# Four products straight into TensorE's accumulator in every second group of states, in place of GpSimd's pair sums

## The reference

```python
def step(h, inputs):
    dt_t, B_t, C_t, x_t = inputs
    dA = jnp.exp(dt_t[..., None] * A)
    h = h * dA + (dt_t * x_t)[..., None] * B_t[:, None, :]
    y = jnp.einsum('bds,bs->bd', h, C_t)
    return (h, y)
```

## Time and profile before

| what | value |
|---|---|
| median of 3 runs | 2714.99 us (2712.98 to 2716.85) |
| profiled execution, its own time | 2713.94 us |
| its span in the trace | 2712.1 us |
| first scan starts, last scan starts | 39.67 us, 336.91 us |
| last `ysum` starts | 342.11 us |
| chunks by their first scan | 39.67, 105.63, 179.19, 259.56 us |
| busy over the whole span | PE 87%, DVE 90%, ACT 85%, POOL 57% |
| granted TensorE clock, mean over the span | 0.952 of full |

### The profile page before, as it was taken

The page is one execution under the profiler, slowest core; times in us unless marked ns, Lnnn a source line. Parts: engine busy times, 40 slices in busy tenths (PEclk is TensorE's granted clock), DMA queues, the critical chain, the costliest instruction groups (busy, mean ns, idle before and its releaser), DMA issues.

```text
span 2712.1 us, 93622 instructions
## 1 busy us (share of the span) xinstructions
PE 2355.8 (87%) x38225; PEld 1247.0 (46%) x38225; DVE 2436.3 (90%) x3370; ACT 2299.3 (85%) x4209; POOL 1535.4 (57%) x2901
## 2 busy tenths in 40 slices
PE   7777587799989998999999999999999999999866
PEld 3444376244444444444444444444444444444345
DVE  5888745799999999999999999999999999999988
ACT  6888544699999999999999999999999999998853
POOL 5878765444664456644664456545664466544544
PEclk8888788699999999999999999999999999999988
DMA  3222233112110111011110101011111101010000
GB/s 111 76 82 74 70 98 108 50 49 64 33 38 31 49 50 47 24 45 44 53 35 34 49 32 55 30 49 41 40 35 50 49 32 41 28 49 11 2 2 16
DMA packets 52141, 127.23 MB, mean 47 GB/s; under 512 B 6017, under 2 KB 40705, under 8 KB 47233
## 3 DMA queue, kind: packets, MB, share of 16 engines
q1 hardware_dynamic: 43329, 113.12, 12.4%
q0 software_dynamic: 2432, 5.08, 0.6%
q10 hardware_dynamic: 5952, 3.04, 0.4%
HBM read 96.09 MB, written 29.18 MB: 46 GB/s over the span
## 4 chain that ended last, share of the span: by engine, by line
PE 39%; issue 18%; ACT 12%; DVE 12%; POOL 11%; DMA 1%; ACTq 0%; SPq 0%; POOLq 0%; DVEq 0%
PE bank L780 12%; PE bank L707 12%; PE bank L791 10%; ACT E L1073 9%; DVE NM L1507 7%; ACT acc L1024 1%; POOL hC L1652 1%; POOL acc L1769 1%; POOL H L1779 1%; PE bank L688 1%; POOL H L1782 1%; POOL smp L1762 1%; ACT UB L1035 1%; PE bank L701 1%; POOL hC L1655 1%
## 5 line engine op out<-in xcount | busy, mean ns | idle before, releaser
L1507 DVE TENSOR_REDUCE NM<-bank 128x1 f32<-128x1024 f32 x1536 | 1798.4, 1206 | 80.1 <-PE bank L780 59.4
L1073 ACT ACTIVATE E<-bank,NM 128x1024 f32<-128x1024 f32 x1536 | 1707.5, 1118 | 165.7 <-DVE NM L1507 139.2
L780 PE MATMUL bank<-KS,QS 72*32 72x512 bf16 x12288 | 960.0, 388 | 163.9 <-ACT E L1073 110.5
L791 PE MATMUL bank<-E,dg 128*32 128x256 f32 x12288 | 926.2, 385 | 1.7 <-ACT acc L1024 1.7
L1831 POOL TENSOR_TENSOR dg<-mask,RZ 128x128 f32<-128x128 f32 x384 | 153.0, 398 | 827.0 <-DVE RZ L1517 726.8
L780 PEld LDWEIGHTS bank<-KS,QS 72*32 72x32 bf16 x12288 | 252.0, 96 | 707.7 <-ACT E L1073 586.1
L791 PEld LDWEIGHTS bank<-E,dg 128*32 128x32 f32 x12288 | 385.1, 111 | 292.9 <-issue 63.0
L1073 ACT ACTIVATION_READ_ACCUMULATOR E<-bank,NM 128x1 f32 x1536 | 310.5, 202 | 0.0
L1769 POOL TENSOR_TENSOR acc<-acc,rel 128x256 f32<-128x256 f32 x384 | 272.4, 730 | 7.8 <-ACT acc L1024 7.8
L707 PE MATMUL bank<-H,ET 128*32 128x129 f32 x6144 | 187.9, 273 | 2.5 <-DVE ET L1448 2.5
L707 PE MATMUL bank<-hT,WL 128*32 128x256 f32 x2304 | 163.3, 387 | 23.0 <-ACT UB L1035 19.4
(11 more groups left out here) (292 smaller groups left out, 2669.3 us busy)
## 6 DMA issues: line engine op xcount, KB each, us to landing
QS<-scratch SPq DMA_DIRECT2D x69, 384.0 KB
KS<-scratch SPq DMA_DIRECT2D x22, 1152.0 KB
scratch<-UB SPq DMA_DIRECT2D x144, 128.0 KB
CB<-crows SPq DMA_DIRECT2D x32, 512.0 KB, 3.7
WL<-in_wl SPq DMA_DIRECT2D x6, 1091.0 KB, 21.3
KS<-scratch SPq DMA_DIRECT2D x6, 384.0 KB
first<-in_fill SPq DMA_DIRECT2D x8, 247.5 KB, 4.0
second<-in_fill SPq DMA_DIRECT2D x8, 247.5 KB, 4.2
```

Source lines behind the costliest of these rows:

```text
L780: inst = PE_.matmul(bank[x % 3][32 * i:32 * i + 32, k * 512:k * 512 + 512], QS[0:72, half % 2, 4 * hq + i, r0:r0 + 32], KS[0:72, b, k, 4 * ...
L791: inst = PE_.matmul(pb(6)[32 * k:32 * k + 32, 256 * grp:256 * grp + 256], dg[:, x // 4 % 3, x % 4, :], E[:, x % NE, :].rearrange("p (i k c ...
L1073: A_.activation(E[:, x % NE, :], bank[x % 3][:, :], ACT.Exp, bias=NM[:, x % 4:x % 4 + 1], accum_out=ZS[:, quad % 3, j:j + 1]).then_inc(s[" ...
L1507: V.tensor_reduce(NM[:, x % 4:x % 4 + 1], bank[x % 3][:, :], AX.X, ALU.max, negate=True).then_inc(s["rowmax"], 1)
```

## The change

The 128 steps are 32 groups of four. In the even groups nothing changes. In the odd ones (`whole`) GpSimd makes no pair sum, and TensorE adds each of the four products itself, five steps after the product's own. Who makes which product stays as it was. There are 32 pair sums fewer, and 32 more identity matmuls (96 in place of 64).

```diff
+def whole(q):
+    return q % 2 == 1
...
+def paired(n):
+
+    return n // 8 * 2 + n % 2 + 1
...
 def summed(n):
-    return n // 4 * 2 + n % 2 + 1
+    return sum(4 if whole(q) else 2 for q in range(n // 4)) + (n % 4 if whole(n // 4) else n % 2) + 1
+
+def sums_at(p):
+    out = []
+    for n in range(max(p - 7, 0), min(p - 2, CSTEPS)):
+        late = 5 if whole(n // 4) else {0: 6, 1: 7}.get(n % 4)
+        if late == p - n:
+            out.append(n)
+    return out
...
-                e.wait_ge(s["two"], summed(n))
+                if whole(n // 4):
+                    name, count = product_of(n)
+                    e.wait_ge(s[name], count)
+                else:
+                    e.wait_ge(s["two"], paired(n))
...
-                for late, at in ((6, 0), (7, 1)):
-                    if 0 <= p - late < CSTEPS and (p - late) % 4 == at:
-                        ysum(p - late)
+                for n in sums_at(p):
+                    ysum(n)
...
-                    e.wait_ge(s["y"], summed(32 * k + 28 + c))
+                    e.wait_ge(s["y"], summed(32 * k + 30 + c))
...
-                    e.wait_ge(s["mulP"], made("POOL", n))
-                    e.wait_ge(s["mulC"], made("DVE", n - 2))
-                    G.tensor_tensor(hC[:, (n - 2) % 8, :], hC[:, (n - 2) % 8, :], hC[:, n % 8, :], ALU.add).then_inc(s["two"], 1)
+                    if not whole(n // 4):
+                        e.wait_ge(s["mulP"], made("POOL", n))
+                        e.wait_ge(s["mulC"], made("DVE", n - 2))
+                        G.tensor_tensor(hC[:, (n - 2) % 8, :], hC[:, (n - 2) % 8, :], hC[:, n % 8, :], ALU.add).then_inc(s["two"], 1)
```

More of the change, by code:

```diff
@@ L101, in carried, with ours @@
     return p // 64 * 32 + p % 32 + 1
+def whole(q):
+    return q % 2 == 1
+def ours(engine, q):
+    if engine == "DVE":
+        return (0, 1)
+    return (2, 3)
 def made(engine, n):
-    ours = (0, 1) if engine == "DVE" else (2, 3)
-    return n // 4 * 2 + sum(i <= n % 4 for i in ours)
+    return sum(len(ours(engine, q)) for q in range(n // 4)) + sum(i <= n % 4 for i in ours(engine, n // 4))
 def product_of(n):
-    engine = "DVE" if n % 4 < 2 else "POOL"
+    engine = "DVE" if n % 4 in ours("DVE", n // 4) else "POOL"
     return ("mulC" if engine == "DVE" else "mulP"), made(engine, n)
+def paired(n):
+    return n // 8 * 2 + n % 2 + 1
 def summed(n):
-    return n // 4 * 2 + n % 2 + 1
+    return sum(4 if whole(q) else 2 for q in range(n // 4)) + (n % 4 if whole(n // 4) else n % 2) + 1
[6 more added lines that the diff above has]
+    return out
 def in_order(engine, k):
@@ L608, in ysum @@
                 k, c = n // 32, n % 2
-                e.wait_ge(s["two"], summed(n))
+                if whole(n // 4):
[3 more added lines that the diff above has]
+                    e.wait_ge(s["two"], paired(n))
                 if n % 32 < 2 and k:
                     e.wait_ge(s["y2"], 2 * (k - 1) + c + 1)
-                PE_.matmul(pb(c), ident[:, :], hC[:, n % 8, :], start=(n % 32 < 2), stop=(n % 32 >= 28)).then_inc(s["y"], 1)
+                PE_.matmul(pb(c), ident[:, :], hC[:, n % 8, :], start=(n % 32 < 2), stop=(n % 32 >= 30)).then_inc(s["y"], 1)
             chosen = {}
@@ L1224, in scan_dve @@
                     expert_dve(e, own, j, x)
-                if 0 <= p - 1 < CSTEPS and (p - 1) % 4 < 2:
+                if 0 <= p - 1 < CSTEPS and product_of(p - 1)[0] == "mulC":
                     mul_c(p - 1)
@@ L1645, in scan_pool @@
                 n = p
-                if 0 <= n < CSTEPS and n % 4 >= 2:
+                if 0 <= n < CSTEPS and product_of(n)[0] == "mulP":
                     g = n // 2
```

## The result

| comparison, on its chip | before, median us | change, median us (lowest to highest) | ratio, 95% interval |
|---|---|---|---|
| first | 2714.36 | 2700.75 (2690.43 to 2702.48) | 0.9944 [0.9929, 0.9959] |
| second (e4_change_again) | 2716.29 | 2696.98 (2695.47 to 2707.57) | 0.9940 [0.9921, 0.9958] |
| third (e14_change_fourth) | 2733.93 | 2720.84 (2717.19 to 2727.56) | 0.9952 [0.9938, 0.9967] |

The first row's median of before is over six runs, the three of the table ahead among them. The change is faster by about 0.55%, 13 to 16 us. The forecast was 7.3 us, half of that. The direction was right.

A forecast was written before the change was run, and what follows sets the result against it. No engine was taken to bound the whole recurrence; a removed pair sum counts only where GpSimd ends a wait. Terms -5.6 - 2.7 + 4.0 - 2.0 - 1.0 + 0 = -7.3 us gave 2707 us; own range 2704 to 2711, wider 2700 to 2714.5.

The forecast's parts named there:

- (a): Starts of chunks 1 and 2: no pair sums ahead of `xa`, 2.8 us won each time, 5.6 us gain.
- (b): Behind those waits at chunks 1 and 2: TensorE's clock stays higher, 0.8 and 1.9 us won, 2.7 us gain.
- (c): Convolution steps: two added `ysum`s a chunk at 0.86 us cost 5.2, less one 1.20 us wait: +4.0 us.
- (d): Gating in chunk 3: VectorE's small operations no longer held up behind GpSimd's pair sums, -2.0 us.
- (e): Transposes of `U`, steps 28 and 29: TensorE less idle ahead, so less `ysum` time at the lower clock, -1.0 us.
- (f): End of the recurrence: four pair sums go, but TensorE does more `ysum`s behind step 121; 0 us.
- (g): Elsewhere: added `ysum`s lie in TensorE's gaps and removed sums in GpSimd's slack; counted as nothing.
- clock rival: Chunk 2, B projection: added `ysum`s keep TensorE's clock up, a 5.27 us wait goes; -12.6 us, 2702; chance 0.17.
- slower rival: TensorE becomes the bound: added `ysum`s on the path, also at steps 17 to 20; +8.9 us, 2723; chance 0.10.

The follow-up runs named there:

- e4_change_again: The change itself, unaltered, run again on the same chip as three other kernels, against the kernel before: ratio 0.9940, 2696.98 us.
- e14_change_fourth: The change itself, unaltered, in a third comparison with the kernel before and a fourth trace: ratio 0.9952, 2720.84 us.
- e2: The change in groups 7 and 15 alone, the other odd groups keeping their pair sums as in the kernel before: ratio 0.9967, 9 us.
- e7: Kernel before without the odd groups' pair sums and with no matmul added, so 32 of 128 products are missing from y: ratio 0.9933, 18 us.
- e6: Kernel before with all its pair sums, plus the 32 matmuls the change adds, fed with zeros: ratio 1.0009, 2.4 us slower, not clear of no change.
- e12: The change in groups 1, 3, 9, 11 and 17 alone, in and just behind the convolution steps, otherwise the kernel before: ratio 0.9993.
- e9: Kernel before with the pair sums of group 19 alone (steps 76 to 79) left out, two of 128 products missing: ratio 0.9979, 5.7 us.
- e10: The change in groups 13, 19 and 21 alone, otherwise the kernel before: ratio 0.9981.
- e1: The change in 11 of its 16 groups; groups 1, 3, 9, 11 and 17 keep their pair sums as in the kernel before: ratio 0.9949.
- e3: The change in groups 25, 27, 29 and 31 alone (last chunk), otherwise the kernel before: ratio 0.9983, 4.6 us.

## Why the prediction was half right

**(a) and (b), the chunk starts: right.** 8.3 us forecast, 8.9 measured, in all four traces to 0.1 us, and e2 gives them alone. The split was less good: 3.6 and 4.7 were forecast for the two chunks and both gave 4.45. The relief is enough for it: e7 adds no matmul and wins the same, with 1.39 us of wait left at `trx` and its transposes there in 0.63 us where they took 0.94. So the clock comes with the shorter wait.

The added matmuls by themselves win 1.3 us in chunk 1 (e6) and nothing in chunk 2, and the most of the 1.3 is not the clock. Scan 36 comes only 0.45 us sooner after scan 35. The other 0.9 us lie between scans 36 and 38, where VectorE's product comes to stand just ahead of a GpSimd sum and no longer just behind one. Before, then e6:

```profile
120.20 1.73 DVE L1203 TENSOR_TENSOR hC<-CB,hs 128x512 f32<-128x512 f32 x1
```

```profile
123.19 0.67 DVE L1205 TENSOR_TENSOR hC<-CB,hs 128x512 f32<-128x512 f32 x1
```

In the change too 0.4 of chunk 1's 4.45 us lie between scans 36 and 38, where this product takes 1.22 us. Step (b) had put all but the sums' 2.8 us down to the clock.

**(c), the convolution steps: the failed step.** Two things were wrong in it, with opposite signs. "GpSimd's relief is worth nothing there but for the 1.20 us wait" was false. It was argued from the earlier trace rows, where TensorE has no gap, but those rows show TensorE as it ran with late chunk starts. +3.9 was forecast in three stages, +2.4 measured (+1.4, +2.15, -1.2), and the groups alone (e12) cost nothing that the time shows. The price of 0.86 us for an added matmul held where it could be read alone (scans 48 to 50); what the relief saves was missing. The other thing is the matmul of step 17, "covered" in the prediction: it cost 0.96 us in chunk 0 and 0.86 in chunk 1, a term of 1.8 us that was put at nothing. The relief's worth in these stages is therefore larger than the 1.5 us by which the sum of (c) is off.

**(d), VectorE behind GpSimd: failed in the gating, true elsewhere.** Scans 100 to 120 take 54.66 us before and 54.77 in the change, so -2.0 was 0: the waits moved. (Over four traces each the means are 54.9 and 54.5, by one trace of before at 55.7 and one of the change at 53.7.) In the change, GpSimd and then VectorE:

```profile
265.96 1.27 POOL L1681 TENSOR_TENSOR hC<-CB,hs 128x512 f32<-128x512 f32 x1 [0.27 <-DVE hs L1247]
```

```profile
255.84 1.18 DVE L1360 TENSOR_TENSOR GM<-GM,cst 128x64 f32<-128x64 f32 x1
...
266.03 1.27 DVE L1360 TENSOR_TENSOR GM<-GM,cst 128x64 f32<-128x64 f32 x1
```

The operation of the earlier trace rows again takes 1.27 us, now beside a product that began 0.07 us ahead of it and ended 0.07 us ahead of its end. The Trainium skill, SBUF — State Buffer, Who interferes with whom, has the second to come blocked for the whole of the first one's instruction; these rows agree, and they show what the prediction's reading of the rule left out, that a product of GpSimd takes the sum's place. In chunk 2 the same relief did win: from scan 78 to 80 e9 is 1.7 to 2.0 us shorter than the traces of before.

**(e), the transposes of U: the number came by luck.** Scans 90 to 100 take 21.2 us before and 20.0 in the change, -1.1 where -1.0 was forecast. But the transposes of `U` (steps 28 and 29) belong to scans 92 to 95, which take 7.65 to 7.82 us before and 7.55 to 7.81 in the change, and e10, which has the group that is summed just ahead of them, takes 21.1 us for scans 90 to 100, as before. All of the 1.1 us is between scans 99 and 100, 3.65 us before and 2.52 in the change. There VectorE has two operations of 128x64; before, both stand behind a GpSimd instruction:

```profile
266.29 1.20 DVE L1329 TENSOR_TENSOR GM<-GL,VT 128x64 f32<-128x64 f32 x1
267.52 1.31 DVE L1331 TENSOR_TENSOR GM<-GM,cst 128x64 f32<-128x64 f32 x1
```

and in the change only the second (1.18 us at 255.84, above):

```profile
255.62 0.20 DVE L1358 TENSOR_TENSOR GM<-GL,VT 128x64 f32<-128x64 f32 x1
```

That is (d)'s mechanism at a place where (d) had counted nothing. e1 and e7 have this gain, e2, e3 and e10 have not, so it goes with the pair sums of group 23 (or of group 5, the only other one that they add).

**(f), the end: mis-sized.** 0 forecast, -1.5 measured (-2.6 in e3). The five `ysum`s come as one block behind the wait, to be read against the earlier trace rows:

```profile
326.14 5.97 PE L642 MATMUL bank<-hC,ident 128*128 128x512 f32 x10 [2.68 <-POOL hC L1685]
331.95 0.38 PE L709 MATMUL bank<-ident,WAX 128*128 128x128 f32 x2
```

and in e3, with a granted clock of 1.00 from 334 to 340 us (in the change it was 0.50 from 326 to 328):

```profile
335.81 4.56 PE L642 MATMUL bank<-hC,ident 128*128 128x512 f32 x10 [2.68 <-POOL hC L1685]
340.21 0.38 PE L709 MATMUL bank<-ident,WAX 128*128 128x128 f32 x2
```

The prediction compared 7.1 us before with 6.8 to 8.5 after, at 1.7 us for each of the first three. They took 4.6 to 6.3 us in all, and the waits of 0.65 and 0.49 us that before had between its last three, for pair sums, are gone. Before's own four traces lie between 6.66 and 7.28 us here.

**(g), the rest: open.** "The removed sums [lie] in GpSimd's slack" was taken as 0; the stages 50 to 66 and 84 to 90 show -1.45 and -1.1. Both lie within the scatter of before's own traces (2.3 and 4.3 us), so what part is real stays open; e10 and e12 put 50 to 66 at -0.3 and -0.7 alone. At one place the words are shown false: scans 78 to 80 are 1.4 to 1.7 us shorter in the change, as the sum of step 78 had been in VectorE's way (e9); scans 80 to 82 give 0.86 of that back.

**The rivals.** The clock rival was nearest in size (-12.6 us), but for a wrong reason, and so by luck: its 5.3 us were a wait that is 2.1 us long in the second trace of before, and the scan behind it came 2.0 to 3.6 us sooner in the three repeats. In its place stand the small gains above: against the terms, (a) and (b) give 0.6 more, (c) 1.5, (f) 1.5, and the stages counted as nothing 2.5, with 1.4 less from (d) and (e) together. Of the slower rival's sum two things held: the price of the matmul, and that the one of step 17 is on the path in chunks 0 and 1.

What stays open: the traces account for 12.1 of the 13 to 16 us. These 12.1 us are a ratio of 0.9955, which lies inside all three intervals of the result, so that a further gain behind the scan is not shown. The time from the last `ysum` on varies from 2367.9 to 2373.1 us in before's own traces. Which of the gains of (c) belong to which pair sum was not tested either, as e12 took five groups at once.

## What to carry to other kernels

Relief of an engine must be priced for the state after the edit: when an earlier wait goes, the next stage meets its partners less ready, and relief that the old trace shows as worthless (no gap) then saves the give-back. Removing one instruction of a pair that blocks another engine gains only if nothing takes its place; half of it mostly moved the collisions (1.6 us won from scan 90 to 120), all of it won 7.8 us there. And profile the same kernel several times before a term rests on one wait: a stage of identical code differed here by up to 4.3 us from trace to trace.

## What was not expected of the hardware

- TensorE's granted clock fell at different instructions in executions of the same program. In chunk 2 it was at 0.51 from 224 us on in one trace and still 1.00 until 228 in another; ahead of the fall TensorE had waited 2.45 and 1.58 us. The trace with a wait of 2.21 us kept the upper level through the projection as well. The stage in which it falls (scans 84 to 90) was 18.74 to 23.03 us long in four traces of the kernel before.
- 32 added matmuls of 128x512, 27.5 us at 0.86 each, cost 2.9 us of the scan against the mean of before's traces and 0.09% [-0.01, 0.19] of the time (e6). The start of chunk 1 was even 1.3 us shorter with them, mostly as a VectorE product no longer met a GpSimd sum.
- A cast of 128x128 by VectorE takes 0.20 us alone (e9) and 1.29 us when it starts 0.06 us behind a GpSimd addition of two 128x512 tiles (before).
- VectorE's product of 128x512 took 1.73 us when it began 0.09 us behind a GpSimd sum (before) and 0.67 when it began 0.16 us ahead of one (e6). An operation of 128x64 that began 0.03 us behind a sum still took 0.20 us (the change, at 255.62), so the order may turn on a few hundredths of a microsecond; that was not tested.
